# A gated cross-attention block in float32 accuracy: the setup and the first row rewritten as one list of work for each engine

## The reference, cut to what matters

```
h     = layernorm(x)
q,k,v = h Wq^T + bq,  ctx Wk^T + bk,  ctx Wv^T + bv        (16 heads of 32)
p     = softmax(clip(q k^T / sqrt(32), -50, 50), masked)
delta = layernorm(rs * (p v Wo^T + bo)) * gamma + beta
x     = x + tanh(g_xattn) * delta
y     = bit_linear(silu(bit_linear(xn, gate_w)) * bit_linear(xn, val_w), out_w)    xn = layernorm(x)
out   = x + tanh(g_ffn) * y
```

## Time and profile before

| | us |
|---|---|
| median of 3 runs (lowest, highest) | 789.89 (789.55, 790.12) |
| the profiled execution, its own time | 790.48 |
| span of its trace, first to last instruction | 788.6 |
| mean granted clock of TensorE | 0.965 of full |
| busy: TensorE, VectorE, ScalarE, GpSimd | 706.3, 627.2, 531.9, 315.9 |
| first gate product of row 0 starts at | 148.1 |

### The profile page before, as it was taken

One profiled execution on the slowest core, in us unless ns is written; L12 is line 12 of the kernel. 1 busy time (PEld: TensorE's weight loads), 2 busy tenths in 40 slices (PEclk: granted clock), 3 DMA queues, 4 the chain that ended last, 5 costly groups with the idle time before them and its releaser, 6 DMA issues.

```text
span 788.6 us, 13489 instructions
## 1 busy us (share of the span) xinstructions
PE 706.3 (90%) x4214; PEld 337.3 (43%) x4214; DVE 627.2 (80%) x1297; ACT 531.9 (67%) x691; POOL 315.9 (40%) x485
## 2 busy tenths in 40 slices
PE   4586755778999999999999999999999999999997
PEld 4342332333444444444444444444444544454443
DVE  6787959389777987798779877987788787778885
ACT  3356866676856885679567865796579657856554
POOL 5100133332455345444454445444634552354340
PEclk9798786799999999999999999999999999999999
DMA  8482276511354426432643354335433543243412
GB/s 293 136 319 84 87 225 138 138 29 41 82 118 96 100 57 133 96 81 69 126 103 80 83 119 105 76 80 120 112 73 80 112 103 67 55 81 81 95 41 67
DMA packets 181182, 82.36 MB, mean 104 GB/s; under 512 B 160262, under 2 KB 160518, under 8 KB 180507
## 3 DMA queue, kind: packets, MB, share of 16 engines
q1 hardware_dynamic: 181146, 81.93, 42.5%
HBM read 39.41 MB, written 10.51 MB: 63 GB/s over the span
## 4 chain that ended last, share of the span: by engine, by line
PE 44%; DVE 29%; issue 10%; ACT 7%; DMA 6%; POOL 3%; SPq 0%; DVEq 0%; POOLq 0%; ACTq 0%
PE psum L1576 17%; PE psum L1542 12%; PE psum L1567 7%; DMA arena<-arena 4%; DVE psum L1106 2%; PE psum L1546 2%; ACT arena L853 2%; DVE delta L1164 1%; DVE stats L1145 1%; DVE arena L1111 1%; DVE stats L1061 1%; DVE xmax L1191 1%; DVE delta L1173 1%; DVE stats L1179 1%; PE psum L1603 1%
## 5 line engine op out<-in xcount | busy, mean ns | idle before, releaser
L1542 PE MATMUL psum<-ternary,xqT 128*128 128x512 f16 x1024 | 260.3, 381 | 3.6 <-DVE xqT L1136 2.5
L1542 PEld LDWEIGHTS psum<-ternary,xqT 128*128 128x128 f16 x1024 | 98.0, 98 | 122.9 <-issue 5.7
L1567 PE MATMUL psum<-ternary,arena 128*128 128x512 f16 x496 | 121.6, 379 | 1.7 <-DMA arena<-arena 1.7
L612 POOL TENSOR_TENSOR rstd<-var_e,minus_half 128x1 f32<-128x1 f32 x64 | 39.8, 623 | 200.3 <-DVE var_e L1157 109.9
L790 ACT ACTIVATE arena<-psum,dequant 128x512 f32<-128x512 f32 x128 | 86.5, 680 | 47.2 <-PE psum L1546 47.1
L1576 PE MATMUL psum<-wo_hi,arena 128*128 128x512 f16 x256 | 84.8, 394 | 9.2 <-DMA arena<-arena 8.2
L1576 PE MATMUL psum<-arena,wq_hi 128*128 128x512 f16 x256 | 77.9, 386 | 7.7 <-ACT arena L844 6.8
L1119 DVE TENSOR_REDUCE hmax<-arena 128x1 f32<-128x1024 f32 x64 | 77.6, 1213 | 0.8
L798 ACT ACTIVATE arena<-arena,round_c,hscale 128x1024 f32<-128x1024 f32 x62 | 73.6, 1237 | 2.1 <-DVE hscale L1131 2.0
L1546 PE MATMUL psum<-bias_parts,inv_rows 128*128 128x512 bf16 x192 | 73.0, 380 | 0.0
L830 ACT ACTIVATE arena<-arena,round_c 128x1024 f16<-128x1024 f32 x62 | 70.9, 1144 | 0.3
(11 more groups left out here) (192 smaller groups left out, 1286.1 us busy)
## 6 DMA issues: line engine op xcount, KB each, us to landing
arena<-in_x SPq DMA_DIRECT2D x64, 256.0 KB, 2.8
out<-arena SPq DMA_DIRECT2D x31, 256.0 KB, 2.3
arena<-in_L_ffn_gate_w SPq DMA_DIRECT2D x4, 1024.0 KB, 10.3
arena<-in_L_ffn_out_w SPq DMA_DIRECT2D x3, 1024.0 KB, 7.9
ternary<-in_L_ffn_val_w SPq DMA_DIRECT2D x2, 1024.0 KB, 10.7
kcur<-k_scratch SPq DMA_DIRECT2D x64, 32.0 KB, 2.2
arena<-arena SPq DMA_TRANSPOSE x106, 3.0
ternary<-in_ctx SPq DMA_DIRECT2D x1, 1024.0 KB, 5.5
```

The source lines that it names most:

```text
L1542: ins = M.matmul(ps[:], xqT[:, t % 2, k, :], w[:, k, cols], start=(k == 0), stop=(k == KC - 1 and not biased))
L1567: ins = M.matmul(psO[:], hidT[t % 2][:, k, :], wo2[:, k, :], start=(k == 0), stop=(k == FC - 1))
```

## The change

1. The first row has its own list, `first_row()`, in the `body` of each of ScalarE, VectorE and TensorE (GpSimd and SyncE have one written into `body`), and the setup ahead of it is reordered in the same manner. The order of products is Wk, Wv, context, keys, values, Wq, Wo (`IN_TURN`) in place of Wk, Wv, context, Wq, Wo, keys, values.
2. The maximum over the partitions is made by TensorE and VectorE: a transpose of the column to a row, a maximum of the row, and a product with a row of ones. The five GpSimd calls go.
3. Row 0 stays on the chip: its four x tiles are loaded at once, its residual tiles too, its keys go from SBUF to the score tile and its values to `vcur` by DMA without DRAM (both are stored to DRAM later for the other rows), and its attention output is transposed by TensorE (`first_c_transpose`), with the halves cut by ScalarE and VectorE.
4. Gate and value weights are transposed chunk by chunk (a group is half a chunk) with a semaphore for each of the two engines that copy. ScalarE copies the even gate groups and all value groups; rounding moves partly from ScalarE to VectorE (gate chunk 3).
5. The value bias is one float32 product of a row of ones with the bias row, in the same accumulation. ScalarE moves keys (with their bias) and values out of PSUM.
6. The output bias is cut into parts by GpSimd on a 128 x 4 tile, and three DMAs write the parts to their rows. ScalarE scales gamma, beta and the output bias table by the tanh values.
7. `project` of row 0's second tile and its statistics are done in the first row's list, not in the first pass of row 0. The transposed input of each row uses `both16[t % 2]`, with a semaphore for each.

The core of the diff:

```diff
+        IN_TURN = [(name, k) for name in ("wk", "wv", "ctx", "keys", "values", "wq", "wo") for k in range(KC)]
-                                     k_dram[head:head + HD, :, row, :]).then_inc(k_loaded.sem, 16)
+                                     keys[head:head + HD, :, row, :]).then_inc(k_loaded.sem, 16)
-                sp.dma_start_transpose(hT_both[:, :, t * P:(t + 1) * P], both16[0]).then_inc(hT_loaded.sem, 16)
+                sp.dma_start_transpose(hT_both[:, :, t * P:(t + 1) * P], both16[t % 2]).then_inc(hT_loaded[t % 2].sem, 16)
@@ SyncE, body
+                if b is FIRST:
+                    values_stored()
+                    sp.wait_ge(s_bostep, 2 * PARTS)
+                    for i in range(PARTS):
+                        at = GROUP * GROUP_OF_PART[i]
+                        sp.dma_start(bo_parts[at:at + 1, :], bo_cut[:, i, :]).then_inc(s_bo, 16)
+                    h_T(1, 0)
+                    normed_x(1, 2)
+                    h_T(1, 1)
+                    normed_x(1, 3)
+                    sp.wait_ge(s_wtr, 4)
+                    load_w(2, 0)
+                    sp.wait_ge(s_wabs, 2 * W_CHUNKS)
+                    sp.dma_start(valb_b[:, :], bcast(val_b[0:F // 2], F // 2)).then_inc(s_vbias, 16)
+                    sp.wait_ge(s_wtr, 6)
+                    load_w(2, 1)
+                    h_T(1, 2)
+                    h_T(1, 3)
+                    for t in range(2):
+                        normed_x(2, t)
+                    sp.wait_ge(s_wtr, W_GROUPS)
+                    load_w(2, 2)
+                    sp.wait_ge(s_wtr, W_GROUPS + 4)
+                    load_w(2, 3)
+                    return
@@ GpSimd
-            def largest_of_all(n):
-                pool.wait_ge(s_amax1, n + 1)
-                G.partition_all_reduce(amax[:, n:n + 1], amax1[:, n:n + 1], P,
-                                       bass.bass_isa.ReduceOp.max).then_inc(s_amax, 1)
@@ ScalarE, body
+                def first_row():
+                    norm(1, 0)
+                    norm(1, 1)
+                    query(0)
+                    query(1)
+                    query(2)
+                    query(3)
+                    for k in range(KC):
+                        high("wo", 1, k, wo_hi)
+                    wait(act, mask_set, a, 1)
+                    exps(range(8))
+                    h_high(1, 0)
+                    h_high(1, 1)
+                    round_w(0, 0)
+                    c_high(0)
+                    c_high(1)
+                    round_w(0, 1)
+                    sum_abs(1, 2)
+                    c_high(2)
+                    c_high(3)
+                    weight_copy(0, 0)
+                    weight_copy(0, 2)
+                    sum_abs(1, 3)
+                    round_input(0, 0)
+                    round_w(0, 2)
+                    norm(1, 2)
+                    norm(1, 3)
+                    h_high(1, 2)
+                    h_high(1, 3)
+                    round_w(1, 0)
+                    inverse_rows(0, 0)
+                    weight_copy(0, 4)
+                    weight_copy(0, 6)
+                    round_w(1, 1)
+                    sum_abs(2, 0)
+                    act.wait_ge(s_vd, 16)
+                    wait(act, v_loaded, 0, 16 * 2)
+                    for g in range(4):
+                        weight_copy(1, g)
+                    sum_abs(2, 1)
+                    for g in range(4, 8):
+                        weight_copy(1, g)
+                    for i in range(2, W_CHUNKS - 1):
+                        sum_abs(2, i)
@@ VectorE, body
+                def first_row():
+                    q_low(0, 0)
+                    q_low(0, 1)
+                    row_max(4)
+                    q_low(0, 2)
+                    scale_up(4)
+                    out_bias_scale()
+                    q_low(0, 3)
+                    values_up()
+                    lows(1, wo_hi, wo_lo)
+                    setup_scales()
+                    projection_scales()
+                    for i in range(NPAIR // 2):
+                        bound(i)
+                    attention_out(0)
+                    attention_out(1)
+                    first_c_low(0)
+                    attention_out(2)
+                    attention_out(3)
+                    first_c_low(1)
+                    weight_clip(0, 0)
+                    statistics(True, False, 0, 0, 0)
+                    weight_clip(0, 1)
+                    new_x(0, 0)
+                    x1_stats(0, 0)
+                    first_c_low(2)
+                    first_c_low(3)
+                    input_scale(0, 0)
+                    weight_sum(1)
+                    x_stats(1, 2)
+                    weight_scale(1)
...
+                    weight_copy(0, 1)
+                    weight_copy(0, 3)
...
+                    weight_clip(0, 2)
+                    xq_T(0, 0)
+                    weight_round(0, 3)
+                    weight_clip(1, 0)
+                    weight_copy(0, 5)
+                    weight_copy(0, 7)
+                    weight_clip(1, 1)
+                    for i in range(W_CHUNKS // 2, W_CHUNKS):
+                        weight_round(1, i)
+                    statistics(True, False, 0, 1, 0)
@@ VectorE, setup (after the context is cleaned)
+            largest(0, s_wq, wq_raw)
...
+            largest(1, s_wo, wo_raw)
...
+            keys_clean(0)
...
+            keys_clean(1)
...
+            row_max(3)
+            scale_up(3)
...
+            values_clean(0)
+            keys_low()
+            weight_sum(0)
+            for t in range(2):
+                x_shift(1, t)
+            lows(0, wq_hi, wq_lo)
+            weight_scale(0)
+            values_clean(1)
@@ TensorE
+            def largest_in_a_row(n):
...
+                M.transpose(row_bank, amax1[:, n:n + 1], eye[:]).then_inc(s_amaxT, 1)
+            def largest_to_all(n):
...
+                M.matmul(all_max[:, n:n + 1], ones[0:1, :], row_max_at[:, n:n + 1], start=True,
+                         stop=True).then_inc(s_amax, 1)
...
+                def first_c_transpose(t):
...
+                    for k in range(KC):
+                        ins = M.transpose(first_c_bank(t)[:, k * P:(k + 1) * P], c_tok[:, t % 2, k * P:(k + 1) * P],
+                                          eye[:])
...
+                def first_row():
+                    query(0)
+                    query(1)
+                    query(2)
+                    query(3)
+                    largest_in_a_row(4)
+                    largest_to_all(4)
+                    for j in range(NPAIR):
+                        scores(j)
+                    weighted(0)
+                    weighted(1)
+                    first_c_transpose(0)
+                    weighted(2)
+                    first_c_transpose(1)
+                    weighted(3)
+                    project(0, 0)
+                    first_c_transpose(2)
+                    first_c_transpose(3)
+                    wait(pe, c_ready, 0, NT)
+                    for g in range(SETUP_BANKS):
+                        weight_transpose(0, g)
+                    wait(pe, d_ready, 0, 1)
+                    project(0, 1)
+                    weight_total(1)
+                    xq_transpose(0, 0)
+                    for g in range(SETUP_BANKS, W_GROUPS):
+                        weight_transpose(0, g)
+                    for g in range(W_GROUPS):
+                        weight_transpose(1, g)
...
+            transposes("ctx", ctx_clean, s_ctxc, 1)
+            largest_in_a_row(0)
+            largest_to_all(0)
+            pe.wait_ge(s_free_act, 3 * KC)
+            keys(0)
+            first_h_transpose(0)
+            largest_in_a_row(1)
+            keys(1)
+            largest_to_all(1)
+            first_h_transpose(1)
+            largest_in_a_row(2)
+            keys(2)
+            largest_to_all(2)
+            first_h_transpose(2)
+            keys(3)
+            first_h_transpose(3)
+            for r in range(KC):
+                values(r)
+                if r == 1:
+                    largest_in_a_row(3)
+                if r == 2:
+                    largest_to_all(3)
+            transposes("wq", wq_raw, s_wq, 16)
+            transposes("wo", wo_raw, s_wo, 16)
+            weight_total(0)
```

704 lines of the change are left out of this document (366 added, 338 removed).

## The result

The changed kernel took 778.22 us, the median of four runs (775.97 to 780.42), where the kernel before took 789.84 beside it: a ratio of 0.985 [0.982, 0.989], 11.6 us faster. The forecast was 775.3 with a range of 767 to 783. The profiled run took 779.99, its span is 778.2; before, 790.48 and 788.6.

What follows compares the result with a forecast made beforehand. The first row was taken as a chain of waits, later rows as TensorE-bound. First gate product 148.1 to 133.5 gains 14.6 us, steady rows 0: profiled 790.48 becomes 775.9, less 0.6 for the median 775.3; range 767 to 783.

Steps and rivals of the forecast that it cites:

- The forecast's own sign of being wrong: Row 0 to steady rows: prediction fails if the 14.6 us lead at the first gate product isn't found at 241.
- Step 1: Setup, keys and values: key products start at 19.4, key scale is there at 51.3 us against 67.8 before.
- Steps 3 to 5: First row, scores through attention to first gate product: scores at 80.4, first projection at 96.7, gate product at 133.5 us.
- the first rival: TensorE at full clock throughout, in first query and second projection too: lead 18.2 us, time 771.7; chance 0.24.
- Step 5: First row's tail, exponentials to first gate product: ScalarE 36.4 us work, 8.8 waits; gate product at 133.5, lead 14.6.
- That absorbs it: Row 0: ScalarE's 3.4 us extra lateness behind TensorE's first product fits its idle 1.1 and 2.7 us before two queries.
- the third rival: ScalarE sets row 0, lead is that of its first silu (about 138.2): 11.2 us, time 778.7; chance 0.12.
- the slower rival: Steady rows: a shared buffer makes a transpose wait behind loads, 3.3 us in each of seven rows: 798.4; chance 0.03.

Runs made afterwards that it cites:

- both orders: Changed kernel with the third out_w load ahead of row 1's input transposes and row 1's first x tiles ahead of the value weights: 774.34 us, ratio 0.9812.

## Why the prediction was right, and where it was off

**The way of working** held: walk the written lists, find who comes last, subtract at the first gate product. The forecast's milestones and the trace's: key products 19.4 and 20.1, end of setup 70.2 and 73.4, scores 80.4 and 81.0, weighted sums 88.0 and 89.9, projection 96.7 and 95.4, first gate product 133.5 and 131.1. Steady rows unchanged, as said. That the time fell into the range is in part luck, though: the first gate product came 2.4 us better than forecast, and behind it 6.2 us of its lead were lost where the forecast lost none. The forecast's own sign of being wrong, a lead of 14.6 that isn't found at 241, came true: it was 12.1 at 226 (238 in the kernel before) and 10.8 at 251.

**Step 1, an unseen queue.** The key scale came at 54.5, not 51.3. The prediction had VectorE wait for the third value product; it waited first, and longer, for x tiles that SyncE had issued behind seven 1 MB loads of weights. The run with x earlier shows both waits, one behind the other.

**Steps 3 to 5, why the gate product came earlier.** The forecast gave ScalarE 45.2 us from the end of the exponentials to its last copy ahead of the gate product: 36.4 of work and 8.8 of waits. In the trace it is 40.4, from 89.0, 2.0 later than forecast, to 129.45, where TensorE's last wait ends, for VectorE's last clip and not for a copy. ScalarE has 34.4 of work in it and 6.1 of waits. The work is 2 us less because neighbouring instructions overlap by about 0.1 us each, which the sum left out for all but the copies. Of the waits, those for the transposed outputs are 1.8 instead of 4.0:

```profile
92.78 0.59 ACT L928 CAST arena<-psum 128x512 f16<-128x512 f32 x1 [0.73 <-PE psum L1803]
94.45 0.59 ACT L928 CAST arena<-psum 128x512 f16<-128x512 f32 x1 [1.09 <-PE psum L1803]
```

The weighted sums in front of them ran at the full level, two groups in 2.10 us, where the forecast took 3.63 from the old trace. The run through DRAM is the counterpart: with its weighted sums at the low level (3.79) these waits were 4.9 and the gate product came at 133.2, where the forecast has 133.5. Of the clock in the query, which was forecast low, this can't be said: it was 1.00 in the first trace of the changed kernel and 0.50 up to 69 in the second, and of the 1.1 us between them 0.4 were left at the gate product. The two traces from 66 to 77:

```profile
66.00:77.00 11.00, 11.00 (x55) 5.32 (x55) 9.18 (x15) 6.10 (x10) 0.00 (x0) 1.00 0.66 207
```

```profile
66.00:77.00 11.00, 11.00 (x48) 5.13 (x47) 9.18 (x15) 5.22 (x8) 0.00 (x0) 0.86 0.63 203
```

Both projections ran at the full level, in part the condition of the first rival. The rule that was weighed there, that the full clock doesn't engage for transposes (the Trainium skill, "TensorE: Matmul & The Clock Gate", Part 4: PE-mode transpose), doesn't hold as it stands: transposes ran at 1.00 here, the sixteen at 99.12 in 1.06 us. But the clock didn't rise behind transposes alone in either trace, as it had at 34 in the kernel before. In the first one the clock rose at 59.8, during float32 products, and stayed at 1.00 through the transposes up to 66.5; in the second it fell at 62.2, when TensorE had nothing to do, stayed at 0.50 through 3.5 us of transposes, and rose at 69.0 inside the query.

In 113 to 131, where transposes are all that TensorE does and it waits between them, the clock was 0.50 (0.59 in the second trace). The run with products in the gaps shows that this cost nothing, as VectorE and ScalarE set the stretch.

**Step 5, the lead after the gate product: the step that failed.** "That absorbs it", the prediction said of ScalarE's being 3.4 us later behind TensorE's first product. It was 6.2 us later: before, the first silu started 1.3 us behind the first gate product, now 7.4. Of these 6.2 ScalarE waited 2.6 for the third out_w chunk. For the first two chunks the prediction had the loads issued at least 8 us before their sums, and they were; for the third it counted the sum and not the load, which was issued at 127.70 and wanted at 132.6. The other 3.5 are the work that it had counted: with both orders, where that wait is gone, the silu is 3.4 us later than before (4.71 against 1.28).

Nor was lateness absorbed as said. From the first silu to the small product of row 0's second tile there are 17.4 to 18.1 us in twelve of the thirteen traces of changed kernels (19.0 in the run with TensorE kept busy, 19.7 in the kernel before), while from the first gate product to it there are 22.0 to 26.9. So row 0 starts from the silu, and ScalarE gives back about 2 us of its lateness in the row, not all of it. That is the mechanism of the third rival. Its number, too, is near: first silu 138.56 where it had about 138.2, lead 10.8 where it had 11.2; 790.48 less 10.8 is 779.7, and the profiled run took 779.99. This closeness is partly chance: a load that the rival didn't have made the silu late, the lead grew to 12.5 in row 0, and 1.3 us of it went in row 1, at the wait of the query for a DMA transpose.

**The maxima were underpriced in the account of before**, though not in the sum. The prediction named one gap of 8.1 us on GpSimd and two VectorE stalls of 4.5 and 5.3; it walked the new lists, which have neither, and so came out right without knowing that the maxima, taken back with as many changes of kind as before, give up 9 to 10 of the 11 us. Order of work, copies by chunk and row 0 on chip are small or depend on them. Not tried was undoing the chunkwise copies alone, the transposed attention outputs by TensorE, or the shared buffer of the slower rival.

## What to carry to other kernels

Look on GpSimd for gaps of "issue" before and behind a partition_all_reduce: a maximum that takes 0.4 us held the chain for 6 to 9 us at each change of kind, and moving it to a transpose, a reduction of one row and a product with ones, or calling it where GpSimd is idle, was most of this gain. When a list is rewritten, follow each DMA queue as one more engine: both waits that the prediction missed were loads behind other entries in SyncE's list, and moving two of its entries gave 4.5 us more. Where two engines are busy 16 and 17 of 18 us, taking 2 us from ScalarE gave nothing, adding 2 us to it cost 2. And follow a lead from point to point behind the place where it was made: here 17.0 us at the first gate product were 10.8 at the first silu.

## What the hardware showed

Instructions of VectorE and GpSimd took longer when they ran side by side. VectorE's timeline at two clips of weights in the changed kernel, and GpSimd's beside it:

```profile
121.50 2.17 DVE L1151 TENSOR_SCALAR ternary<-ternary,wrec 128x2048 f32<-128x2048 f32 x1
123.70 2.06 DVE L1152 TENSOR_SCALAR ternary<-ternary 128x2048 f32<-128x2048 f32 x1
125.68 1.27 DVE L1151 TENSOR_SCALAR ternary<-ternary,wrec 128x2048 f32<-128x2048 f32 x1
```

```profile
120.45 2.14 POOL L708 TENSOR_TENSOR arena<-arena 128x512 f16<-128x512 f32 x1
122.55 2.13 POOL L708 TENSOR_TENSOR x_both<-arena,x_both 128x512 f16<-128x512 f32 x1
124.63 1.18 POOL L736 COPY scur<-att_scale 128x1 f32<-128x1 f32 x1
125.75 1.26 POOL L737 COPY scur<-att_bias 128x1 f32<-128x1 f32 x1
```

The same VectorE instruction takes 2.17 or 1.27 us, and two copies of one column took 1.18 and 1.26 on GpSimd (0.19 and 0.18 in the kernel before, at 147.03 and 147.16). Each of these copies ends within 0.1 us of the VectorE instruction that ran beside it (125.81 and 125.76, 127.01 and 126.95), as if it had waited for that one's end; the rows don't show more. What this costs the first row, in which VectorE is on the path, was not measured by a run of its own.
